# Statistics of the result shared by VectorE and ScalarE, with nine matmuls ahead of the last transposes

## The reference, cut to what matters

```python
out = jnp.einsum('nckhw,ock->nohw', sampled, w) + bias[None, :, None, None]
mean = out.mean(axis=(0, 2, 3), keepdims=True)
var = ((out - mean) ** 2).mean(axis=(0, 2, 3), keepdims=True)
out = (out - mean) * jax.lax.rsqrt(var + BN_EPS)
out = out * gamma[None, :, None, None] + beta[None, :, None, None]
return jax.nn.relu(out)          # and x = x + this
```

## Time and profile before

| | |
|---|---|
| median of 3 runs | 338.06 us (337.65 to 338.84) |
| the profiled execution | 339.78 us, its span 338.0 us |
| busy over the span | PE 264.2 us, PEld 180.7, DVE 276.1, ACT 233.8, POOL 210.1 |
| mean granted clock of TensorE | 0.946 |
| chain that ended last, share | DVE 39%, PE 22%, ACT 17%, issue 7%, POOL 6%, DMA 6% |

### The profile page before, as it was taken

The page is one execution under the profiler, slowest core; times in us unless marked ns, Lnnn a source line. Parts: engine busy times, 40 slices in busy tenths (PEclk is TensorE's granted clock), DMA queues, the critical chain, the costliest instruction groups (busy, mean ns, idle before and its releaser), DMA issues.

```text
span 338.0 us, 16272 instructions
## 1 busy us (share of the span) xinstructions
PE 264.2 (78%) x7273; PEld 180.7 (53%) x7274; DVE 276.1 (82%) x516; ACT 233.8 (69%) x347; POOL 210.1 (62%) x162
## 2 busy tenths in 40 slices
PE   0349996989895987877898898899798999988340
PEld 0336541433434665656666666667566676767230
DVE  4942178881856999999999999999899999999676
ACT  1020175432675799988888899999899999998016
POOL 9100004700405588899889888999899998998400
PEclk9978999799996799999999999999999999999695
DMA  7891000010042121221000002100000210000006
GB/s 253 157 213 31 4 2 0 0 24 4 19 79 30 21 56 22 74 77 25 3 5 4 4 4 109 39 4 6 4 4 4 74 74 5 5 4 4 5 0 248
DMA packets 11956, 14.35 MB, mean 42 GB/s; under 512 B 4269, under 2 KB 7918, under 8 KB 11848
## 3 DMA queue, kind: packets, MB, share of 16 engines
q1 hardware_dynamic: 9852, 11.34, 11.6%
q10 hardware_dynamic: 1952, 1.34, 2.3%
q0 software_dynamic: 80, 0.61, 0.9%
HBM read 4.73 MB, written 2.98 MB: 23 GB/s over the span
## 4 chain that ended last, share of the span: by engine, by line
DVE 39%; PE 22%; ACT 17%; issue 7%; POOL 6%; DMA 6%; DVEq 1%; ACTq 1%; SPq 0%; POOLq 0%
DVE prod L1413 19%; DVE areg L1421 7%; ACT hx L1079 7%; PE ps L608 6%; ACT hx L972 6%; PE ps L829 5%; POOL prod L573 3%; PE ps L695 3%; PE ps L713 3%; DMA hy<-xpad 2%; DMA x_sb<-in_x 2%; DMA preg<-scratch 2%; POOL prod L577 1%; DVE x_sb L1531 1%; PE ps L681 1%
## 5 line engine op out<-in xcount | busy, mean ns | idle before, releaser
L1413 DVE TENSOR_TENSOR prod<-ps,hy 128x480 f32<-128x480 f32 (+1 forms) x256 | 138.1, 601 | 8.4 <-PE ps L829 2.3
L573 POOL TENSOR_TENSOR prod<-prod 128x832 f32<-128x832 f32 x64 | 128.8, 2012 | 17.6 <-DVE prod L1413 15.5
L829 PE MATMUL ps<-zreg,hx 64*64 64x96 f32 x4608 | 123.8, 249 | 18.1 <-DVE prod L1413 10.8
L829 PEld LDWEIGHTS ps<-zreg,hx 64*64 64x64 f32 x4608 | 109.3, 134 | 36.5 <-ACT hx L1079 24.5
L972 ACT ACTIVATE hx<-ps 128x576 f32<-128x576 f32 x129 | 77.0, 650 | 19.6 <-PE ps L713 15.3
L1079 ACT ACTIVATE hx<-hx,rbias 128x1152 f32<-128x1152 f32 x63 | 79.9, 1268 | 0.6 <-ACT hx L972 0.4
L577 POOL TENSOR_TENSOR prod<-prod 128x320 f32<-128x320 f32 x64 | 50.8, 793 | 5.0
L1421 DVE TENSOR_REDUCE areg<-prod 128x64 f32<-128x576 f32 x64 | 48.3, 755 | 2.2 <-POOL prod L577 0.2
L549 POOL TENSOR_TENSOR x_sb<-prod,x_sb 128x512 f32<-128x512 f32 x8 | 10.1, 1269 | 46.8 <-DVE prod L1255 46.8
L713 PE MATMUL ps<-wz,xpad 32*64 32x144 f32 (+1 forms) x1024 | 35.2, 324 | 2.4 <-DVE xpad L1286 1.2
L1074 ACT ACTIVATE zreg<-ps 128x576 f32<-128x576 f32 x56 | 36.9, 660 | 0.0
(11 more groups left out here) (154 smaller groups left out, 267.2 us busy)
## 6 DMA issues: line engine op xcount, KB each, us to landing
zreg<-zreg SPq DMA_DIRECT2D x12, 288.0 KB, 2.4
out<-x_sb SPq DMA_DIRECT2D x7, 256.0 KB, 2.1
x_sb<-in_x SPq DMA_DIRECT2D x3, 512.0 KB, 4.6
preg<-scratch SPq DMA_DIRECT2D x12, 54.0 KB
zreg<-in_pos POOLq DMA_DIRECT2D x1, 528.0 KB, 5.3
x_sb<-in_x SPq DMA_DIRECT2D x2, 256.0 KB, 7.3
scratch<-parts SPq DMA_DIRECT2D x12, 36.0 KB
scratch<-prod SPq DMA_DIRECT2D x10, 36.0 KB
```

The lines of the kernel that those rows point to most:

```text
L573: pool.tensor_tensor(slots[:, :, 0:2 * moved], slots[:, :, 0:2 * moved], slots[:, :, 2 * KEPT:6 * KK], ALU.add).then_inc(half_folded, 1)
L829: return pe.matmul(g_ps(g, h)[u * W:(u + 1) * W, k - TAPS[h][0], :, :], hx[s, (t + u) % 4, k, :], z_sb[s, b, at:at + 3, k * C:(k + 1) * C] ...
L1413: mul = vector.tensor_tensor(pv[:, n0:n1], gv, wv[:, n0:n1], ALU.mult)
```

## The change

Three parts. (1) PE: between the end of `far_rows` and the wait for `acc_final` there are a wait for `g_used` (all weighing of the main loop done) and nine matmuls of 128x384, fp32, into bank 7, whose results are not read. (2) Chunks 0 and 4 are taken from DVE: ACT reads each twice, with `Identity` and with `Square`, each with the accumulator giving the sum over the chunk; the first `Identity` is also the save of chunk 0, in place of L1124, and no longer waits for a `bn_stats`. (3) DVE does six `bn_stats` instead of eight; ahead of the last one it waits for ACT's sums and adds the two chunks' (one small operation), and after `bn_aggr` and L1514 it has one small operation more, which joins its own statistics with ACT's. PE's average matmul now waits for two of ACT's reads (`outt_saved`) instead of one. `out_t` grows by 1024 columns for ACT's unneeded outputs.

```diff
+        sums = sb("sums", [P128, 2, 2])
...
-        out_t = zflat[:, 0:NPIX]
+        out_t = zflat[:, 0:NPIX + 2 * BANK]
...
+        ACT_STATS = (0, 4)
+        SUM_SCALES = (1.0, 1.0 / NPIX)
...
             far_rows(pe, begin, far_tile, far_turn)
 
 
+            pe.wait_ge(g_used, NT + CREDIT)
+            for _ in range(9):
+                pe.matmul(ps[:, 7 * BANK:7 * BANK + 3 * P128], identf[:, :], z_sb[:, 0, 8:10, 0:3 * P128 // 2],
+                          start=True, stop=True)
             pe.wait_ge(acc_final, 1)
...
-            pe.wait_ge(outt_saved, 1)
+            pe.wait_ge(outt_saved, 2)
             pe.wait_ge(bst_ready, 1)
...
-            act.wait_ge(st_ready, 2 * NCH + 1)
-            act.activation(out_t[:, 0:BANK], ps[:, 0:BANK], ACT.Copy).then_inc(outt_saved, 1)
+            for n, c in enumerate(ACT_STATS):
+                act.wait_ge(outt_made, c + 1)
+                of = ps[:, c * BANK:(c + 1) * BANK]
+                act.activation(out_t[:, c * BANK:(c + 1) * BANK], of, ACT.Identity, scale=SUM_SCALES[n],
+                               accum_out=sums[:, n, 0:1]).then_inc(outt_saved, 1)
+                act.activation(out_t[:, NPIX + n * BANK:NPIX + (n + 1) * BANK], of, ACT.Square,
+                               scale=SUM_SCALES[n] ** 0.5, accum_out=sums[:, n, 1:2]).then_inc(sums_ready, 1)
             root(4)
...
-            for c in range(NCH):
+            own = [c for c in range(NCH) if c not in ACT_STATS]
+            for n, c in enumerate(own):
                 vector.wait_ge(outt_made, c + 1)
-                vector.bn_stats(bstats[:, c, :], ps[:, c * BANK:(c + 1) * BANK]).then_inc(st_ready, 1)
-            vector.wait_ge(st_ready, 3 * NCH)
-            chain(vector.bn_aggr(small[:, MVB:MVB + 2], bstats[:, :, :]))
-            vector.scalar_tensor_tensor(col(MVB + 1), col(MVB), col(MVB), col(MVB + 1), ALU.mult, ALU.add)\
-                .then_inc(bst_ready, 1)
+                if c == own[-1]:
+                    vector.wait_ge(sums_ready, len(ACT_STATS))
+                    chain(vector.scalar_tensor_tensor(sums[:, 0, :], sums[:, 0, :], SUM_SCALES[1], sums[:, 1, :],
+                                                      ALU.mult, ALU.add))
+                vector.bn_stats(bstats[:, n, :], ps[:, c * BANK:(c + 1) * BANK]).then_inc(st_ready, 1)
+            vector.wait_ge(st_ready, 2 * NCH + len(own))
+            chain(vector.bn_aggr(small[:, MVB:MVB + 2], bstats[:, 0:len(own), :]))
+            chain(vector.scalar_tensor_tensor(col(MVB + 1), col(MVB), col(MVB), col(MVB + 1), ALU.mult, ALU.add))
+            vector.scalar_tensor_tensor(small[:, MVB:MVB + 2], small[:, MVB:MVB + 2], len(own) / NCH, sums[:, 0, :],
+                                        ALU.mult, ALU.add).then_inc(bst_ready, 1)
```

More of the change, by code:

```diff
@@ L248, in conv_deform_kernel @@
         bst_ready = sem("bst_ready")
+        sums_ready = sem("sums_ready")
         bmean_ready = sem("bmean_ready")
```

## The result

| | before | changed |
|---|---|---|
| median of 22 runs | 337.83 us (335.67 to 340.41) | 341.11 us (338.34 to 344.52) |
| profiled execution, its span | 339.78, 338.0 | 341.01, 339.3 |

The changed kernel is slower: ratio 1.0081, 95% interval 1.0061 to 1.0102. (The ratio leaves disturbed executions out, so it is not quite that of the medians.) The forecast was 341.4 us, from 339.4 to 343.0, and a loss of 3.3 us; the medians differ by 3.3 us, and by the ratio it is 2.7 us.

A forecast was written before the change was run, and what follows sets the result against it. The prediction took the tail to hang on DVE and PE in turn, slow transposes holding DVE's first three chunks. Overrun +4.55 and gain -1.25 made +3.3 us: 338.06 to 341.4 us, range 339.4 to 343.0.

The forecast's parts named there:

- Start of the fill: On PE, behind its loop exit: the nine matmuls start 0.6 us after `first_used`, at 316.1 us.
- Price of a call: One 128x384 matmul of the nine on PE: 0.66 us at the high clock, about 1.3 at the low one.
- rival (c): On PE ahead of the transposes: the nine matmuls fit, no overrun, only the gain left, 336.8 us; chance 0.05.
- Low clock: During PE's nine matmuls: the clock is low for 3.1 us, which adds 1.55 us.
- rival (b): During PE's nine matmuls: the low clock holds longer, 6.5 us, net +4.9 us, 343.0 us; chance 0.18.
- rival (a): During PE's nine matmuls: the clock never drops, or hardly; they take 5.9 us, net +1.7, 339.8 us; chance 0.22.
- What comes back: From first transpose to average matmul: high clock and sharing make it 6.15 us against 7.39, a gain of 1.25.
- The rule on transposes: At PE's transposes: by the skill page all 32 go slowly, 6.8 us; the prediction followed the trace's clock rise instead.
- +4.55: On PE ahead of the transposes: time by which the nine matmuls overrun 319.04 us, when PE was free before.
- -1.25: From first transpose to average matmul: time in us given back by the high clock and the sharing.

The follow-up runs named there:

- early_nine: The changed kernel with its nine matmuls moved straight behind the far tile's sampling, into bank 0: 335.49 us against 337.21 of before, ratio 0.9953.
- fill_only: The kernel before with the nine matmuls alone added, all eight `bn_stats` still on DVE: 340.86 us against 337.53 of before, ratio 1.0090.
- share_only: The changed kernel without its nine matmuls, sharing between DVE and ACT kept: 338.55 us against 337.53 of before, ratio 1.0028.

## Why the prediction was right

**Start of the fill.** Forecast 0.6 us after the far products; measured 0.63 (312.83 less 312.20), and 0.63 in the second profile. DVE's and ACT's loop exits were good stand-ins for PE's.

**Price of a call.** 0.66 and 1.3 forecast; 1.28 at the low clock in the changed kernel, and 9 in 6.07 in early_nine, 0.64 each with some 0.3 for the last one's tail left out. The 16 records for eight calls were the row that decided between this and rival (c).

**Low clock.** The step that was off in size. I took 3.1 us from the transposes' row; it was 6.1 in the first profile (a tail 4.5 us longer than in the first profile of before, near rival (b)'s 4.9) and 3.4 in the second (7.77 us of fill against 7.5). Fill_only had 3.4 too. The reading of the earlier trace rows was at fault: 3.1 us is only what was left of the low clock when the transposes began. From its fall (315.3) to its return (322.1) it had lasted 6.8 us, and a fill that starts soon after the fall meets most of that, as it did in the first profile (312.1 to 318.9, also 6.8). That other executions had only 3.4 was not in the rows, and why a stretch is short or long stays open. So that the median fits a term of 3.1 is in part luck. No profile of the changed kernel had none, as rival (a) has it; run times down to 338.3 leave room for it, but no trace shows one.

**What comes back.** 6.15 us forecast from first transpose to average matmul, 5.90 measured. The first of DVE's chunks came at 1.07 instead of 1.16, and `bn_aggr` took 0.32 instead of 0.37; the operation on the sums held the last statistic back by 0.17 (0.78 between the last two starts, not 0.61) and not by 0.25. Six statistics went as forecast, 0.61 apart. The gain against 7.39 is 1.49, of which by fill_only 0.43 is the sharing and 1.06 the clock. ScalarE's reads were as thin in cover as I put it, but enough: the trace shows for each read 0.60 and an accumulator read of 0.20 that overlaps it by half, 0.59 from one read to the next, so chunk 4's were done at 325.39, 0.44 ahead of DVE's need. No table load stands between Sqrt and Square.

**The rule on transposes.** The Trainium skill, "TensorE: Matmul & The Clock Gate", part 4, says that they don't bring the high clock. In share_only and in the second profile of before it came back during transposes too, with no other matmul since the sampling. The rows were the better guide. What the fill could win by the clock was 1.1 us against the first profile of before (7.39 less 6.33) and 1.5 against the second (7.81).

**Of the sum,** the terms were +4.55 and -1.25. In the second profile of the changed kernel against the first of before they are +4.68 (8.24 less 3.56) and -1.49, together +3.2. That is the pair that fits best: in the first profiles they are +5.99 and -1.49, together +4.5. The mean over both profiles of each kernel is +5.3 and -1.7, together +3.6, so both terms were put too low in size, and the errors cancel in part. The profiled execution was forecast at 343.1 us and took 341.01, because its far products ended 3.3 us earlier; the median doesn't hang on that one execution.

## What to carry to other kernels

Instructions that only keep an engine awake are in order with its real work, so their length has to fit the gap at the slowest clock they may meet, and the gap is measured from where the idle time begins, not from the wait that it precedes. Put them at the start of the idle time: there the same nine matmuls cost nothing and keep the clock up, which has to be seen in the trace, for at the low clock nine calls (1.28 each) would overrun that gap of 5.9 us too. Taking work off one engine pays only where that engine is the bound; here VectorE was held by slow transposes, so sharing its work alone gained nothing until TensorE was fast.

## What the runs showed of the hardware

- The reading of loop bounds and the exit of PE's loop run while queued matmuls do. PE idle from the sampling on needed 0.63 us from `first_used` to its first matmul; with nine calls in front (early_nine), the transposes follow the fill with no gap.
- The accumulator of an activation is a separate instruction of 0.20 us, but two reads of 128x512 with their accumulators start 0.59 us apart, as close as the 0.60 us of one plain read the earlier trace rows.
- The clock can fall while PE is at work: in the second profile of the changed kernel it fell at 316.2, 0.5 us into the fill, after 3 us of idle time before it. The same idle time had brought it down ahead of the fill in the first.
- The end of the main loop moved between 312.1 and 315.6 us from profile to profile, so a change of 1 us in the tail is seen in the trace of the tail and hardly in the run times.
